# Ten transposes of a recurrent kernel, taken from TensorE to a DMA transpose with GpSimd on both sides

## The reference

```python
u = jnp.einsum('bsd,hd->bsh', layernorm(x), W_in) + b_in          # 512 -> 1024
def step(state, u_t):
    s = jnp.tanh(u_t + state * gamma + beta)
    return (s, s)
_, states = jax.lax.scan(step, init, jnp.swapaxes(u, 0, 1))       # 1,024 steps
y = jnp.einsum('bsh,dh->bsd', states, W_out) + b_out              # 1024 -> 512
x1 = x + layernorm(y)

gate = silu((layernorm(x1) @ q(gate_w)) * gate_scale)             # 512 -> 1536
up = (layernorm(x1) @ q(up_w)) * up_scale
z = ((gate * up) @ q(down_w)) * down_scale                        # 1536 -> 512
out = x1 + layernorm(z)                                           # q: float8_e4m3fn and back
```

## Time and profile before

| | us |
|---|---|
| median of 3 runs | 560.37 |
| lowest, highest run | 556.61, 561.68 |
| profiled execution, span from first to last instruction | 556.6 |
| mean granted TensorE clock, of full | 0.994 |

### The profile page before, as it was taken

How to read it: one execution, slowest core, us unless ns; L and a number is a source line. 1 busy time by engine, 2 the same in 40 slices (tenths; PEclk the granted TensorE clock), 3 DMA queues, 4 the chain that set the end, 5 groups by cost and what they waited for, 6 DMA issues and landing times.

```text
span 556.6 us, 11947 instructions
## 1 busy us (share of the span) xinstructions
PE 540.2 (97%) x2958; PEld 457.6 (82%) x2958; DVE 444.8 (80%) x2608; ACT 374.8 (67%) x2317; POOL 228.0 (41%) x372
## 2 busy tenths in 40 slices
PE   8998989999899999999999999999999999999995
PEld 5846769888688888898889888987888887899994
DVE  3699999978797998878987899778988898874414
ACT  3687687864578777877678667876787777762332
POOL 1222446475446541652338222562341321633532
PEclk9999989999999999999999999999999999999998
DMA  8789398991104200120003000300002000200011
GB/s 275 248 268 250 83 226 154 258 158 40 46 13 153 60 1 1 56 80 2 1 2 114 20 1 2 109 6 2 1 2 77 1 2 2 76 2 1 1 39 38
DMA packets 25334, 39.92 MB, mean 72 GB/s; under 512 B 3761, under 2 KB 8497, under 8 KB 25265
## 3 DMA queue, kind: packets, MB, share of 16 engines
q1 hardware_dynamic: 19904, 30.24, 16.7%
q0 software_dynamic: 4608, 8.39, 8.9%
q10 hardware_dynamic: 752, 0.54, 0.3%
HBM read 26.57 MB, written 4.20 MB: 55 GB/s over the span
## 4 chain that ended last, share of the span: by engine, by line
PE 67%; DVE 4%; ACT 1%; POOL 1%; issue 0%; POOLq 0%; DVEq 0%; ACTq 0%
PE gate_up L1131 25%; PE wide L1087 15%; PE wide L1161 13%; PE wide L1056 12%; DVE recur L1231 1%; PE wide L1107 1%; DVE recur_second L1231 1%; ACT pairs L1556 1%; DVE z L1377 0%; DVE stats_z L1245 0%; POOL z L1744 0%; DVE fused L1364 0%; ACT gated L1591 0%; DVE x_lo L1346 0%; POOL norms L1669 0%
## 5 line engine op out<-in xcount | busy, mean ns | idle before, releaser
L1556 ACT ACTIVATE pairs<-recur 128x8 f32<-128x8 f32 x768 | 137.3, 179 | 90.3 <-DVE recur L1231 90.2
L1231 DVE TENSOR_TENSOR_SCAN recur<-recur,pairs 128x16 f32<-128x16 f32 x768 | 151.0, 197 | 48.1 <-ACT pairs L1556 45.8
L1556 ACT ACTIVATE pairs<-recur_second 128x8 f32<-128x8 f32 x768 | 136.8, 178 | 0.0
L1231 DVE TENSOR_TENSOR_SCAN recur_second<-recur_second,pairs 128x16 f32<-128x16 f32 x768 | 133.2, 173 | 0.0
L1754 POOL TENSOR_TENSOR fused_lo<-fused,fused_hi 128x256 fp32r<-128x256 f32 x95 | 70.4, 743 | 127.9 <-ACT fused_hi L1609 126.0
L1087 PE MATMUL wide<-w_out_sb,pairs 128*128 128x512 f32 (+1 forms) x272 | 112.5, 563 | 0.2 <-ACT pairs L1565 0.2
L1056 PE MATMUL wide<-x_norm_t,w_in_sb 128*128 128x256 f32 x448 | 102.7, 382 | 3.7 <-ACT x_norm_t L1507 3.7
L1056 PEld LDWEIGHTS wide<-x_norm_t,w_in_sb 128*128 128x128 f32 x448 | 84.6, 191 | 16.3 <-ACT x_norm_t L1507 4.3
L1087 PEld LDWEIGHTS wide<-w_out_sb,pairs 128*128 128x128 f32 x272 | 75.5, 298 | 25.9 <-ACT pairs L1565 0.7
L1161 PE MATMUL wide<-down_q,fused_hi 128*128 128x512 f32 x192 | 81.7, 425 | 1.9 <-POOL fused_lo L1754 1.9
L1591 ACT ACTIVATE gated<-gate_up,gate_scale_cols 128x128 f32<-128x128 f32 (+1 forms) x169 | 63.4, 378 | 27.0 <-PE gate_up L1131 26.8
(11 more groups left out here) (135 smaller groups left out, 777.2 us busy)
## 6 DMA issues: line engine op xcount, KB each, us to landing
x_res<-x SPq DMA_DIRECT2D x16, 256.0 KB, 3.3
x_in<-x SPq DMA_DIRECT2D x14, 256.0 KB, 4.6
out<-z SPq DMA_DIRECT2D x14, 256.0 KB, 2.5
x_norm_t<-x_t SPq DMA_DIRECT2D x5, 512.0 KB, 4.9
raw_own<-rounders POOLq DMA_DIRECT2D x9, 256.0 KB, 5.2
w_in_sb<-w_in_t SPq DMA_DIRECT2D x4, 512.0 KB, 7.0
w_out_sb<-w_out_t SPq DMA_DIRECT2D x8, 256.0 KB, 5.4
raw_own<-down_w SPq DMA_DIRECT2D x8, 256.0 KB, 4.7
```

Source lines behind the costliest of these rows:

```text
L1231: eng.tensor_tensor_scan(preact_of[b].rearrange("p c k -> p (c k)"), factors_of[b].rearrange("p c k -> p (c k)"), pairs[:, t % RING, colum ...
L1556: ins = eng.activation(pairs[:, t % RING + 1, columns, 0], preact_of[b][:, :, 1], ACT.Tanh)
```

## The change

Normalized x1 of blocks 2 to 6 (`by_planes(n)`) is no longer turned by TensorE. For each tile, 128 tokens by 512 float32:

1. x1_planes: a copy on GpSimd splits each float32 of `x1_norm` into its two 16-bit halves and writes them as two planes of 512 halves into `powers`.
2. x1_turn: a transposing transfer, issued by SyncE, turns the eight squares of 128 by 128 halves into the third slot of `raw_own`.
3. x1_words: a copy on GpSimd joins the halves to words again, into slot b of `raw_own`.

x1_high and x1_low then read that slot in SBUF, not a PSUM bank. There is one buffer for planes and one for turned planes, so a tile's split waits for the landing of the tile before, and its turn for that tile's join. The join waits for the landing, and for x1_low of the same tile of the block before where that went the same way. r_norm of the next block waits for the split and not for t2. down of blocks 2 and later waits, for its bank, for the copy of z of the block before; y of block 7 for the copy of y of block 6; u of block 2 for u copies of block 1 too. Blocks 0, 1 and 7 are still turned by TensorE. In the plan x1_low of those blocks counts as `two_ports`. All due times and most step costs are new.

```diff
-U_STEPS, Y_STEPS, TRANSPOSE_STEPS, GATE_UP_STEPS, DOWN_STEPS, FIRST_U_STEPS, ROUND_STEPS = 7.0, 14.0, 1.0, 3.9, 1.9, 7.4, 2.8
+U_STEPS, Y_STEPS, TRANSPOSE_STEPS, GATE_UP_STEPS, DOWN_STEPS, FIRST_U_STEPS, ROUND_STEPS = 7.14, 14.4, 0.91, 3.876, 1.934, 7.4, 2.77
...
-CHUNKS_PER_BLOCK = [10, 13.5, 13, 10.5, 10, 6, 8.5, 11]
+CHUNKS_FROM = [85.7, 71.1, 340.5, 549.7, 569.7, 933.7, 1034.6, 1071.5]
+CHUNKS_PER_BLOCK = [9.5, 44.5, 18.0, 11.0, 4.5, 7.0, 21.0, 8.5]
...
+TURNED_X1_FROM = 2
+PLANE_STEPS, TURN_LANDS = 3.0, 8.0
 TURNED_FROM = 3
-PACE = 1.05
+PACE = 1.09
...
     def transpose_x1(n, b, after, k):
-        tensor(("t2", n, b), TRANSPOSE_STEPS, [(v, 0.2) for v in rows("r", "r_norm", n, b)] + after, ROWS_TURNED[batch * n + b])
+        if by_planes(n):
+            again = by_planes(n - 1)
+            planes = [(v, 0.2) for v in rows("r", "r_norm", n, b)]
+            if again or b > 0:
+                planes += [(("x1_words", *((n, b - 1) if b > 0 else (n - 1, batch - 1))), 0.0)]
+            side("gpsimd", ("x1_planes", n, b), planes, k, PLANE_STEPS)
+            t.add("sync", ("x1_turn", n, b), ISSUE_STEPS, [(("x1_planes", n, b), 0.2)], 0.0)
+            words = [(("x1_turn", n, b), TURN_LANDS)]
+            if again:
+                words += [(v, 0.2) for v in rows("low", "x1_low", n - 1, b)]
+            side("gpsimd", ("x1_words", n, b), words, k, PLANE_STEPS)
+            turned = ("x1_words", n, b)
+            after = [v for v in after if v[0][0] == "gate_up"]
...
+        x1_planes, x1_turned = powers[:, :].bitcast(U16), raw_own[:, batch, :].bitcast(U16)
+        x1_words = [raw_own[:, b, :] for b in range(batch)]
...
+            def turn_x1():
+                for n in filter(by_planes, range(NB)):
+                    for b in range(batch):
+                        yield at["x1_turn", n, b]
+                        eng.wait_ge(s_x1_planes, plane_turns(n, b))
+                        if plane_turns(n, b) > 1:
+                            eng.wait_ge(s_x1_words, plane_turns(n, b) - 1)
+                        eng.dma_start_transpose(out=x1_turned.rearrange("p (g t) -> p g t", t=P), in_=x1_planes
+                                                ).then_inc(s_x1_turned, 16)
...
-                                if p < LAST - 1:
+                                if p < TURNED_X1_FROM:
                                     eng.wait_ge(s_x1_lo, batch * p + b + 1)
                                 else:
                                     eng.wait_ge(s_z_scaled, rows_through("z", p - 1, b))
...
+                        eng.tensor_copy(x1_planes.rearrange("p (v d) -> p d v", v=2),
+                                        x1_norm[:, b, :].bitcast(U16).rearrange("p (d v) -> p d v", v=2)).then_inc(s_x1_planes, 1)
...
+                        eng.wait_ge(s_x1_turned, 16 * plane_turns(n, b))
+                        if by_planes(n - 1):
+                            eng.wait_ge(s_x1_lo, batch * (n - 1) + b + 1)
+                        eng.tensor_copy(x1_words[b].bitcast(U16).rearrange("p (c v) -> p c v", v=2),
+                                        x1_turned.rearrange("p (v c) -> p c v", v=2)).then_inc(s_x1_words, 1)
```

More of the change, by code:

```diff
@@ L165 @@
 TWO_CHAINS_FROM = 2
+LAST_BLOCK = 7
 LAST_CHUNK = 11
@@ L274, in project_u @@
                 after += [(v, 0.2) for v in rows("y", "y_copy", n - 2, m)]
+                if n == 2:
+                    after += [(("u_copy", 1, m + 2, q), 0.2) for q in range(4)]
             if n == 1 and m < 2:
@@ L297, in project_y @@
                 else:
-                    after += [(v, 0.2) for v in rows("low", "x1_low", n - 1, b)]
+                    after += [(v, 0.2) for v in rows("y", "y_copy", n - 1, b)]
                 if (n, b) == (0, 1):
@@ L317, in project_y @@
         side("gpsimd", ("r_root", n, b), [(("r_whole", n, b), 0.2)], k, ROOT_STEPS)
+        read = [(("x1_planes" if by_planes(n - 1) else "t2", n - 1, b), 0.3)] if n > 0 else []
         for name in rows("r", "r_norm", n, b):
-            side("vector", name, [(("r_root", n, b), BEHIND_POOL)] + ([(("t2", n - 1, b), 0.3)] if n > 0 else []), k, two_ports=True)
+            side("vector", name, [(("r_root", n, b), BEHIND_POOL)] + read, k, two_ports=True)
         side("gpsimd", ("x1_shift", n, b), [(v, 0.2) for v in rows("r", "r_norm", n, b)] + [(("y_shift", n, b), 0.0)], k + 20,
@@ L323, in transpose_x1 @@
     def transpose_x1(n, b, after, k):
-        tensor(("t2", n, b), TRANSPOSE_STEPS, [(v, 0.2) for v in rows("r", "r_norm", n, b)] + after, ROWS_TURNED[batch * n + b])
+        if by_planes(n):
[11 more added lines that the diff above has]
+            after = [v for v in after if v[0][0] == "gate_up"]
+        else:
+            tensor(("t2", n, b), TRANSPOSE_STEPS, [(v, 0.2) for v in rows("r", "r_norm", n, b)] + after, ROWS_TURNED[batch * n + b])
+            turned, after = ("t2", n, b), []
         for h in range(2):
-            side("scalar", ("x1_high", n, b, h), [(("t2", n, b), 0.5)], k)
+            side("scalar", ("x1_high", n, b, h), [(turned, 0.5)] + after, k)
         for name in rows("low", "x1_low", n, b):
-            side("vector", name, [(("t2", n, b), 0.5)] + [(v, 0.4) for v in pair("x1_high", n, b)], k)
+            side("vector", name, [(turned, 0.5)] + [(v, 0.4) for v in pair("x1_high", n, b)], k, two_ports=by_planes(n))
     def gate_up(p, i, after, k):
@@ L830, in x1_bank, with turned_on_tensor, plane_turns, wait_x1_read @@
         def x1_bank(n, b):
-            return wide[b] if n >= LAST - 1 else wide[2 + b]
+            return wide[b] if n == LAST else wide[2 + b]
+        def turned_on_tensor(n, b):
+            return batch * sum(not by_planes(m) for m in range(n)) + b + 1
+        def plane_turns(n, b):
+            return batch * sum(by_planes(m) for m in range(n)) + b + 1
+        def wait_x1_read(eng, n, b):
+            if by_planes(n):
+                eng.wait_ge(s_x1_planes, plane_turns(n, b))
+            else:
+                eng.wait_ge(s_t2, turned_on_tensor(n, b))
+        def last_raw_use(r):
+            return max(i for i in range(NP) if raw_of[i] == r)
         def x_bank(b):
```

62 lines of the change are left out of this document (47 added, 15 removed).

## The result

The kernel before takes 559.39 us in these runs (556.61 to 561.68), the changed one 579.12 us (578.02 to 579.7): 1.0351 times as long, 95% interval 1.0303 to 1.0398. The forecast was 559.5 us with a range to 569; the measured time lies 20 us above it.

A forecast was written before the change was run, and what follows sets the result against it. Block 6 was taken to bound the kernel: gate_up start 469.2, less 5.1, plus 82.5 behind it, 1 of other work and 8.2 closing gave 555.8 us, scaled to 559.6 and called 559.5; range 552 to 569 us.

The forecast's parts named there:

- The split: GpSimd's copy of each tile into 16-bit halves: taken as 1.38 us, with bounds of 0.69 and 3.0 us.
- late-turn rival: Landings beyond 5.6 us hold GpSimd's join, low parts and TensorE; scaled 572 us at a 6.9 us landing; chance 0.15.
- The turn: SyncE's transposing transfer of 256 KB within SBUF: landing taken as 3.5 us, range 2.5 to 6.9.
- a landing within about 4 us: At GpSimd's join: the plan leaves about 4 us after the issue, so such a landing costs its queue nothing.
- Block 6 decides: Block 6's longer way to its feed-forward sets the end, within a few microseconds of today; chance 0.52.
- the 82.5 us behind G: Chunks 67.2, last y 14.4 and last transposes 0.87 us, said not to be movable ahead of block 6's gate_up.
- G: Start of block 6's gate_up: from 464.2 to 469.2 us, less 5.1 us; expected at 464 +- 2 us after TensorE idle.
- The way through blocks 2 to 5: The longer way of x1 there got no term in the sum; TensorE was read as never idle from 144 us.
- The 4.35 us of TensorE: TensorE's work saved by dropping the transposes of blocks 2 to 6, 0.87 us for each block's eight.
- The due steps: Reordered dues shift work between blocks, sum unchanged; truer step costs should place copies where products are ready.
- 4.6 us of lateness: Recurrence up to step 896: twelve scan distances above 0.6 us, the excess beyond 0.44 each, expected mostly to go.
- Port collisions: VectorE and GpSimd block each other at SBUF, 7 us of recurrence: 561.5 us, scaled 565; chance 0.08.

The follow-up runs named there:

- the short split: Changed kernel with the split's loops reordered so that GpSimd writes plane by plane, contiguously; 572.42 us, 1.0254 of the kernel before.
- both_only6: Kernel before, TensorE transposes kept, plus split by planes, turn and join in block 6 alone, x1_high waiting for the join; 560.08 us, 1.0012.
- both_ways: Kernel before, TensorE transposes kept, plus split by planes, turn and join in blocks 2 to 6, x1_high waiting for the join; 567.79 us, 1.0164.
- both_to5: Kernel before, TensorE transposes kept, plus split by planes, turn and join in blocks 2 to 5, x1_high waiting for the join; 568.87 us, 1.0174.
- b_quarter: Kernel before with three of four TensorE transposes per tile of blocks 2 to 6 left out; 556.88 us, 0.9962.
- both_quarter: both_ways with three of four TensorE transposes per tile of blocks 2 to 6 left out; 568.79 us, 1.0191 of the kernel before.
- b_new_dues: Kernel before with only the change's five lists of due steps; 568.74 us, 1.0186.
- e1_old_plan: Changed kernel with the split by planes and the due steps, step costs and pace of the kernel before; 575.63 us, 1.0331 of the kernel before.

## Why the prediction was wrong

**The split: a term mis-sized.** It was 1.38 us, with 3.0 as bound; it is 4.79. The bound came from the dearest element in the earlier trace rows, as if the cost were the operation's. It is the order of the writes', and no row of before had 2-byte writes 1,024 bytes apart. The diff showed both loops: the join (1.15 us, taken as 1.38) writes in order, the split doesn't. This is 1.0% of the time under the new lists. The late-turn rival named the mechanism rightly, a low part behind GpSimd and TensorE waiting for it, and also that a long split has the same effect. But it hung its chance of 0.15 on a landing above 5.6 us, and the landing was 3.1 (5.0 at most).

**The turn: right in its size.** Taken as 3.5 us from 2.5 to 6.9, it is 3.1 us, near the plain transfer's 3.3 of the earlier trace rows. That a landing within about 4 us would cost GpSimd's queue nothing did not hold: it waits 17.8 us at the joins, and 12.1 us with the short split. With the short split TensorE waits only 0.5 us for low parts, so these waits are not what costs. By the Trainium skill's 1,309 ns per square (VectorE: DVE Perf Modes, the three transpose paths), the eight squares one after another would take 10.5 us, an estimate from that figure. This case's transfers of 3.1 us (5.0 at most) don't bear it out.

**"Block 6 decides": failed.** The step was the sentence that the 82.5 us behind G can't be moved ahead of it. They held 6.98 us of the last y's first half, and both_only6 runs most of that ahead of G. Up to the join the longer way was well counted: it ends 6.4 us after the last normalized piece (461.39 to 467.78 us), 6.6 were forecast. G comes 12.2 us after that piece, not 7.5, since y stands ahead of it; it moves by 9.3 us and the time by nothing that can be told (1.0012). In the changed kernel itself G is at 489.64 us, not at 464, behind block 5's backlog and without idle time ahead: what delays it comes from the blocks before.

**The way through blocks 2 to 5: priced at nothing, costs 9 to 10 us.** This is the step that failed first: the term was left out, and both_ways and both_to5 show it (1.0164 and 1.0174), latency and the plan's order for it together. The prediction read that TensorE is never idle from 144 to 438 us and took that as cover. It is the opposite: with no idle time, whatever opens a hole pushes all later work. The question to ask at each handover was which products TensorE would do while x1 is on its way. At 227 us the two chunks of gate_up were the filler, and x1 being late takes away the filler itself.

**The 4.35 us of TensorE: mostly right in the old kernel, not seen beside the longer way.** b_quarter shows two thirds of such a gain (2.1 of 3.3 us); both_quarter shows none once x1 is late, within its intervals.

**The due steps: failed.** "The sum of the work is unchanged" is true and says nothing of holes. I expected most of 4.6 us of lateness to go. In the changed kernel VectorE's copies of y wait no more after 144 us, as forecast, but the steps of the recurrence take 0.470 us instead of 0.458. With the lists alone the scans did become a little tighter (493.2 us in b_new_dues), and the feed-forward paid with 11 us of backlog. Of the two chains, the recurrence that was read in the earlier trace rows was not the one that ended last.

**Port collisions: mechanism seen, price near nothing alone.** The forecast gave them 0.08 and 565 us. They lengthen single steps by up to 1.2 us (304.37 to 306.02 us in e1_old_plan, beyond 0.44). By its own terms the rival's sum is 561.8 us, not 561.5: 555.8 + 7, less the 1 us that it held already.

The parts don't add up: 1.9% for the lists on the old way and 1.6% for the way on the old plan would be 3.5%, without the split; together they are 2.5%. That interaction is measured, not explained; the changed kernel also has other step costs and pace and 4.35 us less on TensorE. How the 2.5% divide between lists and way in the changed kernel itself is open.

## What to carry to other kernels

In this kernel a longer latency ahead of an engine that never idled was not covered by its load. So look at each handover for the products that fill the time, and ask whether they depend on the very thing that comes late. For such a copy on GpSimd, price the order of its writes before its operation; the same halves by planes cost 1.04 us instead of 4.79. And count a saving on the full engine only where that engine stays full.

## What the runs showed of the hardware

A GpSimd copy of 1,024 16-bit elements per partition takes 1.04 us with writes in order, 1.15 with reads alternating between two planes, 1.32 with writes in steps of 4 bytes, and 4.7 to 4.9 us where successive writes lie 1,024 bytes apart. A transposing transfer of 256 KB from SBUF to SBUF takes 1.26 us to issue and 3.1 us from issue to landing, both in the median (5.0 us at most). After 3.34 us without work TensorE's granted clock was 0.50 for about three microseconds, where the five stretches of 58 to 62 us before had shown 1.00.

The same hole at block 2's handover, 3.2 us without work, was followed by 0.50 in both_ways and by 1.00 in both_to5, whose programs are alike up to there. Granted clock by the microsecond (TensorE's busy time and instructions first), both_ways, then both_to5:

```profile
233.00:234.00 1.00, 1.00 (x3) 0.50 0.00 0
...
234.00:235.00 1.00, 1.00 (x4) 1.00 0.00 0
```

So the length of a hole alone did not tell whether the clock fell. Beside 9 us of loss in both it weighs little: both_ways is at 1.0164, both_to5 at 1.0174.
